# Edge weights and node numbers read from PSUM in the message stage of a graph-attention layer

## The reference, cut to what matters

```python
att = ex / (denom + EPS)                                  # softmax over the edges of a source node, 8 heads
msg = att[:, :, None] * jnp.transpose(h_e[:, dst], (1, 0, 2))
out = jax.ops.segment_sum(msg, src, num_segments=N)       # (2500, 8 * 64)
```

## Time and profile before

| what | us |
|---|---|
| median of three runs | 3604.73 |
| lowest, highest of the three | 3603.67, 3625.55 |
| the profiled execution, whole time | 3586.76 |
| its span, first to last instruction | 3584.8 |
| from the first gather to the last gather's start in `gather_messages` | 2096.9 to 3113.6 |

### The profile page before, as it was taken

How to read it: one execution, slowest core, us unless ns; L and a number is a source line. 1 busy time by engine, 2 the same in 40 slices (tenths; PEclk the granted TensorE clock), 3 DMA queues, 4 the chain that set the end, 5 groups by cost and what they waited for, 6 DMA issues and landing times. The chain is left out here.

```text
span 3584.8 us, 65271 instructions
## 1 busy us (share of the span) xinstructions
PE 2740.9 (76%) x17311; PEld 1764.0 (49%) x17312; DVE 2248.0 (63%) x4027; ACT 1448.0 (40%) x2941; POOL 1651.8 (46%) x1562
## 2 busy tenths in 40 slices
PE   2599887989999989989991057777777777779892
PEld 2366544666666666666661034444444444477440
DVE  3667635777777777777772967777777777742111
ACT  1233315888888888888882010000000000033220
POOL 1133204444444444444440047777777777612112
PEclk9799988999999999999996579999999999959996
DMA  3012134555555555555555035666666665641124
GB/s 115 18 61 63 56 110 124 143 142 144 142 142 144 143 142 144 143 142 144 143 136 157 0 101 165 173 175 172 174 174 174 173 174 174 164 138 48 62 77 134
DMA packets 181565, 461.62 MB, mean 129 GB/s; under 512 B 50534, under 2 KB 66338, under 8 KB 180739
## 3 DMA queue, kind: packets, MB, share of 16 engines
q0 software_dynamic: 116400, 372.54, 37.2%
q1 hardware_dynamic: 55105, 83.86, 7.5%
q10 hardware_dynamic: 10002, 4.53, 0.5%
HBM read 413.88 MB, written 46.86 MB: 129 GB/s over the span
## 5 line engine op out<-in xcount | busy, mean ns | idle before, releaser
L1313 POOL DMA_INDIRECT rows_e<-message_rows,edge_dst x672 | 809.8, 1205 | 431.6 <-ACTq L1286 222.9
L1047 POOL DMA_INDIRECT rows_v<-target_rows,edge_dst x672 | 639.0, 951 | 684.0 <-DVE w L1073 577.1
L1355 PE MATMUL ps_sum<-messages,node_onehot 128*125 128x512 f32 x1344 | 745.9, 643 | 243.6 <-DVE messages L1331 154.9
L1073 DVE TENSOR_TENSOR w<-rows_v,ps_u 128x520 f32<-128x520 f32 x672 | 468.0, 696 | 376.1 <-issue 284.4
L1164 ACT ACTIVATE slope<-w_abs,a_abs,minus_prd 128x256 f32<-128x256 f32 x1344 | 697.8, 593 | 0.1
L1111 PE MATMUL ps_u<-edge_space,source_onehot_t 125*128 x4032 | 593.6, 280 | 133.5 <-DVE w L1073 131.0
L1331 DVE TENSOR_TENSOR messages<-rows_e,edge_space 128x1024 f32<-128x1024 f32 x336 | 411.6, 1225 | 246.9 <-DMA rows_e<-message_rows,edge_dst 246.5
L1111 PEld LDWEIGHTS ps_u<-edge_space,source_onehot_t 125*128 125x128 bf16 x4032 | 362.9, 97 | 357.8 <-issue 279.0
L1356 PEld LDWEIGHTS ps_den<-edge_space,node_onehot 128*125 128x125 f32 x1344 | 254.5, 189 | 329.3 <-issue 329.3
L1678 ACT COPY gate_t<-ps_count 128x32 f32<-128x32 f32 x1 | 0.2, 186 | 1030.6 <-PE ps_count L1611 1030.6
L1086 DVE TENSOR_TENSOR slope<-w_abs,slope 128x1024 f32<-128x1024 f32 x336 | 409.4, 1218 | 4.2 <-ACT slope L1164 4.2
(11 more groups left out here) (380 smaller groups left out, 2943.9 us busy)
## 6 DMA issues: line engine op xcount, KB each, us to landing
scores<-score SPq DMA_DIRECT2D x1344, 8.0 KB
edge_space<-in_L_ffn_w_dram SPq DMA_DIRECT2D x24, 512.0 KB, 4.7
rows_v<-target_rows,edge_dst POOLq DMA_INDIRECT x672
rows_e<-message_rows,edge_dst POOLq DMA_INDIRECT x672
source_parts<-edge_space SPq DMA_DIRECT2D x20, 380.9 KB
edge_space<-source_parts SPq DMA_DIRECT2D x4, 1904.3 KB
token_rows_out<-token_y SPq DMA_DIRECT2D x27, 256.0 KB, 2.7
edge_space<-scores SPq DMA_DIRECT2D x2, 2688.0 KB, 28.2
```

Source lines behind the costliest of these rows:

```text
L1047: nc.gpsimd.indirect_dma_start(rows[q][:, j, :], None, tab_v, bass.IndirectOffsetOnAxis(ap=edge["dst"][:, tile:tile + 1], axis=0)).then_in ...
L1073: v.tensor_tensor(w[q][:, j, :].rearrange("p (a b) -> p a b", a=2), rows[q][:, j, :].rearrange("p (a b) -> p a b", a=2), ps_u[:, :, 0:HALF ...
L1313: nc.gpsimd.indirect_dma_start(rows[q][:, j, :], None, tab_e, bass.IndirectOffsetOnAxis(ap=edge["dst"][:, tile:tile + 1], axis=0)).then_in ...
L1355: nc.tensor.matmul(ps_sum[h][:, :], onehot[h][:, j, :], messages[h][:, j, :], start=j == 0, stop=j == GROUP - 1)
```

## The change

Two PSUM banks `ps_beside` are taken. Each holds in its first 16 columns the weights of one group, and in the next 125 the row of node numbers. VectorE copies the node numbers into both at the start of the stage, ahead of its two memsets. ScalarE copies the 128 x 16 weights of group n into bank n % 2, once the messages of group n - 2 are made. VectorE waits for that copy ahead of the one-hot of group n, and its two products then read one operand from SBUF and one from PSUM. The matmul of line 1356 still reads the weights from SBUF. All eight PSUM banks are in use then.

```diff
--- before.py
+++ after.py
@@ -1295,8 +1295,13 @@
         onehot = [sb(f"node_onehot{h}", [P, GROUP, L]) for h in range(BUFS)]
         ps_sum = [ctx.enter_context(nc.psum_tensor(f"ps_sum{h}", [L, F], F32)) for h in range(BUFS)]
         ps_den = [ctx.enter_context(nc.psum_tensor(f"ps_den{h}", [L, 512], F32)) for h in range(BUFS)]
+        PAIR = GROUP * HEADS
+        ps_beside = [ctx.enter_context(nc.psum_tensor(f"ps_beside{h}", [P, 512], F32)) for h in range(2)]
+        pair_weights = [one[:, 0:PAIR] for one in ps_beside]
+        node_row = [one[:, PAIR:PAIR + L] for one in ps_beside]
 
         messages_set, summed, added = (sem(n) for n in ("messages_set", "e_summed", "e_added"))
+        rows_laid, weights_laid = sem("node_rows_laid"), sem("pair_weights_laid")
         gathered = [sem(f"e_gathered{q}") for q in range(TURN)]
         link_s = sem("gather_link")
         tile_weights = weights.rearrange("p c i h -> p (c i) h")
@@ -1317,6 +1322,10 @@
         def _(dve):
             v = nc.vector
             link = linker(dve, link_s)
+            for h in range(2):
+                ins = v.tensor_copy(node_row[h], row[:, 0:L])
+            ins.then_inc(rows_laid, 1)
+            dve.wait_ge(rows_laid, 1)
             v.memset(denominators[:, :, :], 0.0)
             link(v.memset(sums[:, :, :], 0.0))
 
@@ -1324,13 +1333,13 @@
 
                 h = q % BUFS
                 at_least(dve, summed, n - BUFS + 1)
-                v.tensor_tensor(onehot[h][:, :, :], row[:, 0:L].unsqueeze(1).broadcast_to([P, GROUP, L]),
+                at_least(dve, weights_laid, n + 1)
+                v.tensor_tensor(onehot[h][:, :, :], node_row[q % 2].unsqueeze(1).broadcast_to([P, GROUP, L]),
                                 edge["local"][:, DS(n * GROUP, GROUP)].unsqueeze(2).broadcast_to([P, GROUP, L]), ALU.is_equal)
                 at_least(dve, gathered[q], turn * (16 * GROUP) + 16 * GROUP)
-                w = tile_weights[:, DS(n * GROUP, GROUP), :].rearrange("p j h -> p (j h)")
                 v.tensor_tensor(messages[h][:, :, :].rearrange("p j (h d) -> p (j h) d", d=D),
                                 rows[q][:, :, :].rearrange("p j (h d) -> p (j h) d", d=D),
-                                w.unsqueeze(2).broadcast_to([P, GROUP * HEADS, D]), ALU.mult).then_inc(messages_set, 1)
+                                pair_weights[q % 2].unsqueeze(2).broadcast_to([P, PAIR, D]), ALU.mult).then_inc(messages_set, 1)
 
             def add_up(n, q, turn):
 
@@ -1359,6 +1368,16 @@
                 ins.then_inc(summed, 1)
 
             in_turns(nc.tensor, TURNS, ((0, add_edges),), TURN)
+
+        @block.scalar
+        def _(act):
+            act.wait_ge(rows_laid, 1)
+
+            def lay_weights(n, q, turn):
+                at_least(act, messages_set, n - 1)
+                nc.scalar.copy(pair_weights[q % 2], tile_weights[:, DS(n * GROUP, GROUP), :].rearrange("p j h -> p (j h)")).then_inc(weights_laid, 1)
+
+            in_turns(nc.scalar, TURNS, ((0, lay_weights),), TURN)
 
 
 def route_and_share(nc, a, const, ffn, x_sb, sums, denominators, spare, raw_space, tokens, tab_x, lists):
```

## The result

| what | us |
|---|---|
| the change, median of four runs (lowest, highest) | 3697.52 (3690.14, 3708.90) |
| the kernel before on the same chip, four runs | 3613.85 (3603.67, 3625.55) |
| ratio, with its 95% interval | 1.0233 [1.0184, 1.0282] |
| the profiled execution: whole time, span | 3708.90, 3707.0 |

The change is slower by 2.3%, where a gain of 4.7% was forecast. The page's first lines, with the earlier trace rows to compare: GpSimd is busy for less time than before, VectorE for about as much, and TensorE, with the same work, is busy longer.

A forecast was written before the change was run, and what follows sets the result against it. GpSimd's gather issue was taken to bound the message stage; -171.4 us for the stretching and +3 us for a longer start wait gave -168, so 3604.7 us becomes 3437 us (-4.7%), range 3412 to 3480.

The forecast's parts named there:

- What bounds the kernel: Message stage: GpSimd's issue of two gathers sets the pace, 3.02 us a group, without waiting for other engines.
- Removed, the stretching, -171.4 us: Message stage: 672 gathers drop from 1.205 to 0.950 us beside a product with one PSUM operand, all on the path.
- The PSUM operand at no cost: VectorE's products in the message stage: reading one operand from PSUM adds nothing; bounds 0 and +1.07 us a product.
- The rival of half rate: VectorE's product: the PSUM broadcast runs at half rate, product 2.29 us, kernel slower by 67 us, 3672 us; chance 3%.
- nothing changes: Rival for the message stage's gathers: stretching has another cause than the second SBUF operand, time stays 3605 us; chance 4%.
- The copy and the wait at no cost: Message stage: ScalarE's 0.19 us weight copy and VectorE's wait for it put nothing on the path.
- What is next late: Message stage: at the new 2.51 us pitch VectorE (2.15), TensorE (2.31 us a group) and DMA (209 GB/s) have room.
- the four waits of the earlier trace: Near the message stage's start: GpSimd's 5.4 us of waits for products in four places, to grow by about 3 us.
- The transfers' rival: Message stage: sustained row transfers hold part of the gain, 191 GB/s, pitch 2.74 us, 3511 us; chance 7%.
- The rival on the slower side: VectorE's product in the message stage: PSUM broadcast at half rate makes VectorE the pace, 3672 us; chance 3%.
- None of the three: The prediction's rivals: nothing changes (4%), transfers hold part of the gain (7%), PSUM broadcast at half rate (3%).

The follow-up runs named there:

- e1: The change with ScalarE's copies and VectorE's wait kept, but one-hot and product reading SBUF as before; 3617.26 us, 1.0006 of the kernel before.
- e2: The change with VectorE itself copying the weights to PSUM, ScalarE having no part; 3706.25 us, 1.0253 of the kernel before.
- e12: The change itself, unaltered, on a chip without stalls; 3313.27 us, 0.9489 of the kernel before.
- e5: The change with gathers fetching rows of 1 KB instead of 2 KB from the seventh group on; 3682.56 us, 1.0251 of the kernel before.
- e6: The change with one gather per group instead of two from the seventh group on; 3299.41 us, 0.9184 of the kernel before.
- e20: The change with GpSimd only three groups ahead instead of six, on a chip that stalls; 3707.69 us, 1.0289 of the kernel before.
- e9: The change with a GpSimd memset of 1024 columns ahead of each group's gathers; 3585.52 us, 1.0292 of the kernel before.
- e10: The change with a GpSimd memset of 512 columns ahead of each group's gathers; 3445.36 us, 0.9888 of the kernel before.
- e14: The change with GpSimd's first gather waiting for VectorE's first operation of the stage; 3326.60 us, 0.9528 of the kernel before.
- e18: The change with a GpSimd memset of 512 columns per group, as in e10, run again; 3450.89 us, 0.9913 of the kernel before.
- e19: The change with GpSimd's late first gather, as in e14, run again on another chip; 3328.24 us, 0.9564 of the kernel before.
- e11: The change with GpSimd only three groups ahead instead of six, on a chip without stalls; 3322.49 us, 0.9521 of the kernel before.

## Why the prediction was wrong

- **What bounds the kernel**, GpSimd's issue at 3.02 us a group: right. e1 and e2, on one chip, differ in the gather's mean, 1216 and 948 ns, and on chips without stalls the pitch follows: 2.50 us in e12.
- **Removed, the stretching, -171.4 us:** right in mechanism and size. The mean of line 1313 (now 1318) went from 1205 to 948 ns, and lies between 945 and 952 in every profile with the operand in PSUM. The Trainium skill's sentence on the probe (SBUF — State Buffer, section "Who interferes with whom"), by which a two-tensor operation would not hold up GpSimd's DMAs, is not borne out here (1216 ns with two SBUF operands in e1, 948 with one); the same section's sentence on contention for reads is. That the whole of it lies on the path was right on D and E only: 3480.5 - 3314.0 = 166.5 us and 3492.9 - 3313.3 = 179.6, where the sum said 168.
- **The PSUM operand at no cost:** right, 1209 to 1222 ns against 1225. The fixed cost that the prediction quoted from the Trainium skill (VectorE: DVE Perf Modes, section on the TRN2 errata), an estimate of 0.065 us more for a PSUM source, doesn't show. The rival of half rate is out. So is "nothing changes".
- **The copy and the wait at no cost:** right (e1, 1.0006 [0.9988, 1.0024]; 176 ns against the 186 taken).
- **"What is next late":** this is the step that failed, in its conclusion "So the pitch of 2.51 has room on every engine". TensorE was measured by its busy time, VectorE by the distance of two products at a place where the signals came on time, and both had room. The forecast took TensorE's signal always to come with the end of its matmuls. On chip A that failed about once in five groups, 337 us in all. VectorE, at 2.15 us a group between the stalls instead of the 2.51 of the pitch, made up only a part of it: the stage took 1104.8 us where 845 was forecast, and the kernel 84 us more than before in the medians instead of 168 less. The rows that gave VectorE's 2.15 us come from 2204 us, right behind the stalls of the kernel before, and the four waits of the earlier trace rows were read as "VectorE had fallen behind" and priced at 3 us; what made it fall behind was not looked up. The timeline at the 4.18 us among them shows idle of over 4 us ahead of the sums, three times.
- **The transfers' rival:** out; 210 GB/s held for 680 us (e12), and half the bytes changed nothing where it stalls (e5).
- **The rival on the slower side** was the wrong one. None of the three was a wait between VectorE and TensorE, and the 3% for "slower" had no room for it.
- **One number for the chip:** the forecast has one time. On D and E it holds as a ratio (0.9531 and 0.9489, where 3437/3604.7 = 0.9535 was forecast), on the others the sign turns.

What is shown: the stall is in TensorE's signals and not in its work, as far as the starts of its matmuls show it; the steady row of stalls came only with unstretched gathers at two per group (with e1's stretched ones 9 stalls, with e6's single ones 1), and neither the bytes (e5), the handshake (e1, e2) nor a lead of GpSimd cut to three groups (e20) makes or cures it; it comes on some chips, every time, and not on others; and on the same chips TensorE's signals are late in the score stage too. What stays open: why the signals are late, what in those chips makes them so, and whether the number of gathers, their signals (S2) or their pace matters. On chips that stall, neither a pause of GpSimd of over half a microsecond nor the late start could be tried, since e9, e10, e14, e18 and e19 met the other kind. The Trainium skill (Perfetto Trace Analysis, section "Tensor Engine Instruction (MATMUL, LD_WEIGHTS)") says that a matmul's end is an estimate of the profiler's, and that its semaphore is pushed only when PSUM has acknowledged all bytes. By that the late step could be the write's acknowledgement as well as the signal's way; no run here tells the two apart. The starts of the next groups, 1.08 us a tile, show only that the array itself went on.

A version that beats both kernels on every chip was not found. On D and E none of the versions that compute everything beats the change itself.

## What to carry to other kernels

An engine's room is not a loop's room: where two engines hand to each other, price the signal too, from the places in the trace where it was late, however few, and look up what lies behind each odd wait near a stage's start before giving it 3 us. A stage that no change touches tells whether two runs met the same kind of chip. A stretched instruction can be what keeps such a ring in step; take it away and the next thing in the ring shows. And run the unaltered change beside every cure on the same chip: two cures here (e10, e11) looked good on a chip that had no need of them.

## What the runs showed of the hardware

- In the message stage with two SBUF operands in VectorE's product a gather of GpSimd takes 1.2 us on the mean and up to 2.0; with one operand in PSUM 0.95, in 672 of 672. VectorE's product pays nothing for PSUM (1209 to 1222 ns against 1225).
- TensorE's semaphore updates can come over 5 us after the matmuls' modelled end (2409.75 against 2404.27), three of them 0.1 us apart: 66 or 67 stalls in each of six profiles with unstretched gathers at two per group on A, B and C, none in eleven on D and E. In the score stage they come a median 0.35 us (line 1111, the records that are there) and 1.05 us (line 1138) behind the matmuls' modelled end on A, and 0.01 and 0.02 us behind it on E.
- The same kernel (before) takes 3589 to 3617 us on some chips and 3481 to 3493 on others; the score stage alone takes 1317 to 1333 us on the first kind and 1219 to 1221 on the second.
- A stall's end goes with GpSimd's last gather (a median 2.10 us behind its end with whole rows, 1.96 with half ones) and not with the last bytes, which in the medians come 0.33 us after it with whole rows and 0.48 us before it with half ones.
- A memset of 115 ns between two indirect gathers of GpSimd costs nothing: it fits into the 0.30 us that lie between them. One of 542 ns adds 0.41 us to a group (2.50 to 2.91).
- After 3.58 us without work (in the changed kernel, ahead of 2412.16 us) TensorE ran at the lower of its two levels, and the next group took 4.27 us instead of 2.15. VectorE's next sums waited only a little for it, 0.37 us in the timeline shown.
